# Delta-rule recurrence: four scaling operations read PSUM, and the time rows of k are computed in two other places

## What is computed

```python
q = _causal_dwconv_silu(x @ Wq.T, qcw, qcb).reshape(Bb, Tt, H, DK)
k = _causal_dwconv_silu(x @ Wk.T, kcw, kcb).reshape(Bb, Tt, H, DK) * SCALE
v = _causal_dwconv_silu(x @ Wv.T, vcw, vcb).reshape(Bb, Tt, H, DV)
a = jax.nn.sigmoid(x @ Wa.T + ba).reshape(Bb, Tt, H, DV)
beta = jax.nn.sigmoid(x @ Wb.T + bb)

def step(S, inp):
    qt, kt, vt, at, bt = inp
    err = jnp.einsum('bhij,bhj->bhi', S, kt) - vt
    S = at[..., None] * S - bt[..., None, None] * (err[..., None] * kt[:, :, None, :])
    o = jnp.einsum('bhij,bhj->bhi', S, qt)
    return (S, o)
...
_, o = lax.scan(step, S0, xs)
```

## Time and profile before

| | us |
|---|---|
| median of 3 runs | 3798.8 (3794.1 to 3808.3) |
| the profiled execution | 3802.3 |
| its span | 3800.5 |
| of it the recurrence | about 149 to 2237 |

### The profile page before, as it was taken

One profiled execution on the slowest core, in us unless ns is written; L12 is line 12 of the kernel. 1 busy time (PEld: TensorE's weight loads), 2 busy tenths in 40 slices (PEclk: granted clock), 3 DMA queues, 4 the chain that ended last, 5 costly groups with the idle time before them and its releaser, 6 DMA issues. The chain is left out here.

```text
span 3800.5 us, 141833 instructions
## 1 busy us (share of the span) xinstructions
PE 3221.9 (85%) x61117; PEld 2418.8 (64%) x61117; DVE 2951.2 (78%) x6533; ACT 1981.8 (52%) x4486; POOL 2230.6 (59%) x2825
## 2 busy tenths in 40 slices
PE   3688898888888888889888845689999799889989
PEld 2567676767767676767677644556666477656765
DVE  4488888888888888889888942178888688738884
ACT  2434444444444444444444323258887699629972
POOL 1377778787877777787877744320101388418860
PEclk7889999999999998999999966899999899999999
DMA  2111111111111111111111115100000012101111
GB/s 76 34 43 41 35 52 30 52 34 45 42 45 42 45 41 37 50 30 49 31 40 40 40 31 149 40 1 2 2 2 2 23 35 44 29 20 29 43 32 28
DMA packets 156019, 141.03 MB, mean 37 GB/s; under 512 B 64976, under 2 KB 108236, under 8 KB 155138
## 3 DMA queue, kind: packets, MB, share of 16 engines
q1 hardware_dynamic: 153090, 129.25, 12.5%
q0 software_dynamic: 2304, 2.71, 0.2%
HBM read 96.12 MB, written 16.82 MB: 30 GB/s over the span
## 5 line engine op out<-in xcount | busy, mean ns | idle before, releaser
L1327 DVE TENSOR_TENSOR a_tmp<-a_h,banks 128x128 f32<-128x128 f32 (+6 forms) x896 | 435.7, 486 | 28.7
L1333 DVE TENSOR_REDUCE a_h<-a_tmp 128x64 f32<-128x128 f32 (+6 forms) x896 | 432.1, 482 | 8.8
L1012 POOL TENSOR_TENSOR a_st<-a_st,a_ab 128x512 f32<-128x512 f32 x252 | 313.6, 1277 | 0.0
L820 ACT ACTIVATE a_kq<-banks 128x512 f32<-128x512 f32 (+2 forms) x160 | 88.3, 552 | 426.6 <-PE banks L556 426.6
L2207 ACT ACTIVATE c_s<-c_s,c_low 128x384 f32<-128x384 f32 (+1 forms) x512 | 266.3, 579 | 19.1 <-DVE c_low L2151 13.6
L1027 POOL TENSOR_TENSOR a_h<-a_h,a_a 128x128 f32<-128x128 f32 (+3 forms) x256 | 141.3, 552 | 228.4 <-DVE a_h L1333 225.6
L2252 POOL TENSOR_TENSOR c_qm<-c_qT,c_heads 128x512 f32<-128x512 f32 x32 | 33.3, 1040 | 396.2 <-PE banks L2076 395.9
L2151 DVE CUSTOM_DVE_ANT_0 c_s<-banks,c_band 128x384 f32<-128x384 f32 (+1 forms) x512 | 245.4, 517 | 23.5 <-PE banks L2076 23.5
L556 PE MATMUL banks<-a_xseg,a_w_q 128*128 128x128 f32 x2048 | 253.4, 278 | 9.0 <-ACT a_kq L820 8.5
L556 PE MATMUL banks<-a_xseg,a_w_k 128*128 128x128 f32 x2048 | 243.0, 276 | 17.1 <-DMA a_xseg<-xn 17.1
L556 PEld LDWEIGHTS banks<-a_xseg,a_w_q 128*128 128x128 f32 x2048 | 235.8, 190 | 21.6 <-ACT a_kq L820 15.4
(11 more groups left out here) (326 smaller groups left out, 8917.5 us busy)
## 6 DMA issues: line engine op xcount, KB each, us to landing
a_ab<-decays SPq DMA_DIRECT2D x512, 128.0 KB, 3.1
d_Vs<-d_V SPq DMA_DIRECT2D x128, 128.0 KB, 2.4
sent<-k_nothing SPq DMA_DIRECT2D x40, 64.5 KB, 2.6
b_xe<-sent SPq DMA_DIRECT2D x8, 322.5 KB, 3.5
a_xseg<-xn SPq DMA_DIRECT2D x32, 70.0 KB, 2.8
a_xrow<-in_L_attn_x SPq DMA_DIRECT2D x128, 16.0 KB, 1.8
x<-a_xrow SPq DMA_DIRECT2D x128, 16.0 KB, 1.8
back<-k_nothing SPq DMA_DIRECT2D x32, 64.0 KB, 1.6
```

The source lines that it names most:

```text
L1012: e.tensor_tensor(sv, sv, self.ab[:, 8 * n:8 * n + 8, :], ALU.mult).then_inc(*self.s_decay.at((g, n)))
L1327: e.tensor_tensor(prod, both, gram, ALU.mult).then_inc(*step.at((g, t, "product")))
L1333: e.tensor_reduce(self.results(ch, t), prod, AX.X, ALU.add).then_inc(*step.at((g, t, "w")))
```

## The change

It does four things, all in `DeltaRule`.

1. Gram rows. The rows of bank 2 are kept in another order, q of step t-1 before k of step t, and only in the columns that the products read: columns 0 to 7 for the steps of the first half, 8 to 15 for those of the second. Two copies of 112 and 120 elements take the place of two of 240 and 256. The column of outputs O moves to the front of H, so that one sum still writes both results.
2. Factors. In the columns of bank 2 that are now free ScalarE copies the dk of rows 0 to 3 and 8 to 11 (`act_factors`, two copies of 128 elements), before the Gram rows of the same chunk. It waits for GpSimd's dk and for the last chunk's line 1391. GpSimd waits for this copy before it overwrites dk, where it waited for the multiplications.
3. Products. The multiplications of lines 1297 and 1363 read the factor in PSUM and write their product to unread columns of bank 3; the subtraction and addition behind them (lines 1302 and 1366) read it there. Line 1297 now waits for the factors and for the gate rows of its chunk.
4. Time rows. `pe_time_rows` and `act_time_rows` leave the beginning of a segment. Half 0 stands ahead of the second chunk's `pe_cross`, half 1 between the two halves of v's projection. The last segment has none.

The core of the diff:

```diff
@@ layouts
-            self.W = [self.H[:, :, ch * SEG:(ch + 1) * SEG] for ch in range(NCK)]
-            self.Wx, self.O = self.H[:, :, 2 * SEG:2 * SEG + CK], self.H[:, :, 2 * SEG + CK:]
+            self.O, self.Wx = self.H[:, :, 0:CK], self.H[:, :, CK + 2 * SEG:]
+            self.W = [self.H[:, :, CK + ch * SEG:CK + (ch + 1) * SEG] for ch in range(NCK)]
...
-        self.gbank = c.bank(2).rearrange("p (t z j) -> p t z j", z=2, j=CK)
+        self.gbank = c.bank(2).rearrange("p (r j) -> p r j", j=CK)
+        self.factor = [self.gbank[:, 2 * HC * h:2 * HC * (h + 1), HC - HC * h:CK - HC * h].rearrange("p r (i t) -> p r i t", t=HAND)
+                       for h in range(2)]
+        self.scaled = c.bank(3)[:, HAND * 32:2 * HAND * 32].rearrange("p (r i t) -> p r i t", i=2, t=HAND)
@@ act_gram_bank, act_factors
-        e.activation(self.gbank[:, 0:CK - 1, 0, :], self.g2[:, 1:CK, 0, js], ACT.Copy)
-        e.activation(self.gbank[:, :, 1, :], self.g2[:, :, 1, js], ACT.Copy).then_inc(*self.s_gbank.at(g))
+        e.activation(self.gbank[:, 0:2 * HC - 2, 0:HC], rows[:, 1:2 * HC - 1, c0:c0 + HC], ACT.Copy)
+        e.activation(self.gbank[:, 2 * HC:2 * CK - 1, HC:], rows[:, 2 * HC + 1:, c0 + HC:c0 + CK], ACT.Copy).then_inc(*self.s_gbank.at(g))
+
+    def act_factors(self, e, q, g):
+
+        q.wait_ge(self.s_dk, (g, 1))
+        if g:
+            q.wait_ge(self.s_step, (g - 1, "last", "q"))
+        for h in range(2):
+            t = e.activation(self.factor[h], self.by_pairs(self.dk[:, :, h * HC:h * HC + HAND]), ACT.Copy)
+        t.then_inc(*self.s_factor.at(g))
@@ pool_prepare
-            q.wait_ge(self.s_prep, (g - 1, "mul"))
+            q.wait_ge(self.s_factor, g - 1)
             q.wait_ge(self.s_rest, (g - 1, "late"))
-            q.wait_ge(self.s_mid, (g - 1, "mul"))
@@ dve_steps
-        q.wait_ge(self.s_dk, (g, 1))
-        first = P2[:, :, 0:HAND, 0]
-        e.tensor_tensor(first, first, self.dk[:, :, 0:HAND], ALU.mult).then_inc(*self.s_prep.at((g, "mul")))
+        q.wait_ge(self.s_factor, g)
+        q.wait_ge(self.s_abank, g)
+        pairs = self.by_pairs
+        e.tensor_tensor(self.scaled, pairs(P2[:, :, 0:HAND, 0]), self.factor[0], ALU.mult).then_inc(*self.s_prep.at((g, "mul")))
...
-        e.tensor_tensor(Wc[:, :, c0:c0 + HAND], self.bv[:, :, c0:c0 + HAND], first,
+        e.tensor_tensor(pairs(Wc[:, :, c0:c0 + HAND]), pairs(self.bv[:, :, c0:c0 + HAND]), self.scaled,
                         ALU.subtract).then_inc(*self.s_prep.at((g, "sub")))
         q.wait_ge(self.s_prep, (g, "sub"))
         q.wait_ge(self.s_gbank, g)
-        q.wait_ge(self.s_abank, g)
@@ dve_cross
-        e.tensor_tensor(x, x, self.dk[:, :, HC:HC + HAND], ALU.mult).then_inc(*self.s_mid.at((g, "mul")))
+        e.tensor_tensor(self.scaled, pairs(self.X[:, :, HC:HC + HAND, 0]), self.factor[1], ALU.mult).then_inc(*self.s_mid.at((g, "mul")))
...
-        e.tensor_tensor(self.history(ch, HC)[:, :, HC:HC + HAND], self.P2[:, :, HC:HC + HAND, 0], x, ALU.add).then_inc(
+        e.tensor_tensor(pairs(self.history(ch, HC)[:, :, HC:HC + HAND]), pairs(self.P2[:, :, HC:HC + HAND, 0]), self.scaled, ALU.add).then_inc(
@@ tensor
-            for n in range(2):
-                self.pe_time_rows(e, q, s, n)
...
+                self.pe_time_rows(e, q, s, 0)
             self.pe_cross(e, q, s, 1)
             if more:
                 self.pe_project_rows(e, q, "v", nxt, 0)
                 self.pe_past_state(e, q, g + 2)
+                self.pe_time_rows(e, q, s, 1)
                 self.pe_project_rows(e, q, "v", nxt, 1)
```

More of the change, by code:

```diff
@@ L502, in __init__ @@
         self.s_y, self.s_scaled, self.s_cum, self.s_bv, self.s_bg = (sig(n) for n in ("y", "scaled_o", "cum", "bv", "bg"))
+        self.s_factor = sig("factor")
         self.s_p2, self.s_prep, self.s_step, self.s_wt, self.s_st, self.s_o = (
@@ L526, in results @@
     def results(self, ch, t):
-        w, o = self.first_column(ch, t + 1) + t, 2 * SEG + CK + t - 1
-        return self.H[:, :, w:o + 1:o - w].rearrange("p i z -> p z i")
+        w, o = self.first_column(ch, t + 1) + t, t - 1
+        return self.H[:, :, o:w + 1:w - o].rearrange("p i y -> p y i")
     def ubank(self, n):
@@ L886, in act_gram_bank @@
         s, ch = divmod(g, 2)
-        js = slice(ch * CK, (ch + 1) * CK)
+        c0, rows = ch * CK, self.g2[:].rearrange("p t z j -> p (t z) j")
         q.wait_ge(self.s_bg, (s, ch))
@@ L890, in act_gram_bank, with by_pairs @@
             q.wait_ge(self.s_step, (g - 1, "last", "q"))
-        e.activation(self.gbank[:, 0:CK - 1, 0, :], self.g2[:, 1:CK, 0, js], ACT.Copy)
-        e.activation(self.gbank[:, :, 1, :], self.g2[:, :, 1, js], ACT.Copy).then_inc(*self.s_gbank.at(g))
+        e.activation(self.gbank[:, 0:2 * HC - 2, 0:HC], rows[:, 1:2 * HC - 1, c0:c0 + HC], ACT.Copy)
+        e.activation(self.gbank[:, 2 * HC:2 * CK - 1, HC:], rows[:, 2 * HC + 1:, c0 + HC:c0 + CK], ACT.Copy).then_inc(*self.s_gbank.at(g))
+    def by_pairs(self, x):
+        return x.rearrange("p (r i) t -> p r i t", i=2)
+    def act_factors(self, e, q, g):
[5 more added lines that the diff above has]
+        t.then_inc(*self.s_factor.at(g))
     def act_out(self, e, q, s):
@@ L946, in scalar @@
         self.act_cross_gram(e, q, 0)
+        self.act_factors(e, q, 0)
         self.act_gram_bank(e, q, 0)
@@ L956, in scalar @@
                     self.act_project_rows(e, q, "a", nxt, half)
-            for n in range(2):
-                self.act_time_rows(e, q, s, n)
             if older >= 0:
@@ L969, in scalar @@
                     self.act_project(e, q, "q", nxt, part)
+            self.act_factors(e, q, g + 1)
             self.act_gram_bank(e, q, g + 1)
@@ L983, in scalar @@
                     self.act_next_gram(e, q, s, n)
+                self.act_time_rows(e, q, s, 0)
             if old >= 0:
@@ L987, in scalar @@
                 self.act_cross_gram(e, q, nxt)
-                for half in range(2):
-                    self.act_project_rows(e, q, "v", nxt, half)
-            if more:
+                self.act_project_rows(e, q, "v", nxt, 0)
+                self.act_time_rows(e, q, s, 1)
+                self.act_project_rows(e, q, "v", nxt, 1)
+                self.act_factors(e, q, g + 2)
                 self.act_gram_bank(e, q, g + 2)
@@ L1037, in past_part @@
     def past_part(self):
-        return self.H[:, :, SEG:SEG + CK]
+        return self.H[:, :, CK + SEG:CK + SEG + CK]
     def pool_past(self, e, q, s):
@@ L1046, in pool_past @@
         q.wait_ge(self.s_wm, 2 * s + 1)
-        e.tensor_tensor(self.past_part(), self.H[:, :, 0:CK], by, ALU.mult).then_inc(*self.s_past.at(s))
+        e.tensor_tensor(self.past_part(), self.W[0][:, :, 0:CK], by, ALU.mult).then_inc(*self.s_past.at(s))
     def pool_clear(self, e, q, s):
@@ L1313, in dve_steps @@
             both = hist[:, :, lo:t + 1].rearrange("p (o i) j -> p o i j", o=1).broadcast_to([P, 2, 32, t + 1 - lo])
-            gram = self.gbank[:, t - 1, :, lo:t + 1].rearrange("p z (o j) -> p z o j", o=1).broadcast_to([P, 2, 32, t + 1 - lo])
+            gram = self.gbank[:, 2 * t - 2:2 * t, lo:t + 1].rearrange("p y (o j) -> p y o j", o=1).broadcast_to([P, 2, 32, t + 1 - lo])
             if t == lo + 1 and lo:
@@ L1337, in dve_cross @@
     def dve_cross(self, e, q, s, ch):
-        g, x = 2 * s + ch, self.X[:, :, HC:HC + HAND, 0]
+        g, pairs = 2 * s + ch, self.by_pairs
         q.wait_ge(self.s_step, (g, HC - 1, "w"))
@@ L1389, in dve_state @@
             e.transpose(self.Wt[:].rearrange("p x i -> p i x"), Wc).then_inc(*self.s_wt.at(g))
-        gq = self.gbank[:, CK - 1, 1, HC:].rearrange("p (o j) -> p o j", o=1).broadcast_to([P, 32, HC])
+        gq = self.gbank[:, 2 * CK - 2, HC:].rearrange("p (o j) -> p o j", o=1).broadcast_to([P, 32, HC])
         e.tensor_tensor(self.tmp[:, 1, :, 0:HC], Wc[:, :, c0 + HC:row], gq, ALU.mult).then_inc(*self.s_step.at((g, "last", "q")))
```

2 lines of the change are left out of this document (1 added, 1 removed).

## The result

The changed kernel takes 3707.2 us (median of 4 runs, 3700.7 to 3721.1) against 3798.9 us before: a ratio of 0.976, 95% interval 0.973 to 0.979. That is 92 us faster, where 159 us were forecast.

What follows compares the result with a forecast made beforehand. Bound by VectorE's own work plus two round trips through TensorE. Gains 82 (operations) + 119 (waits) - 25 (new wait) = 176 us, less 15 for longer waits, 161: 3802 to 3641, said 3640 us; range 3605 to 3715.

Steps and rivals of the forecast that it cites:

- The four operations: VectorE lines 1297, 1302, 1363, 1366 each fall to 289 ns with one PSUM operand: 82 us over 64 chunks.
- The reason given, waiting for GpSimd: VectorE's operations with two SBUF operands run long because they wait inside the instruction for GpSimd, not from computing.
- Time rows and the clock: Moved time rows fill TensorE's idle time before second cross and line 691; full clock at both, first-chunk waits 0.
- What is then late: VectorE's waits left after the move: 0.96 us at second cross, 0.67 at second past chunk, 52 us over 32 segments.
- the 0.96 us of the full-clock row: VectorE's wait behind the second chunk's cross at 457.38, run at full clock, taken as what stays there.
- gone: 119: VectorE's waits for cross and past-chunk matmuls fall from 170.8 us to 52, a gain of 119 us.
- rival 1: TensorE's clock stays at the lower level behind shorter gaps, costing 50 us: 3690 us, 15%.
- longer waits in some segments that I see no reason to lose: Mean segment 0.48 us longer than the one followed: 15 us in all, taken off the 176 us gain.
- Rival 2: Time rows become late ahead of the second cross, where only 0.35 us are idle; 32 us lost: 3672 us, 12%.
- The new wait: VectorE waits before line 1297 for ScalarE's factors and gate rows: 0.8 us in 31 first chunks, 25 us lost.
- the prediction's path: Check between line 1348's starts: 29.3 us first to second chunk, 30.8 second to first.
- the forecast of 60.1 us a segment: Path check of the recurrence: 60.1 us a segment against 65.2 in the mean, 160 us over 31.5 segments.

Runs made afterwards that it cites:

- e1: The changed kernel with both halves of k's time rows back at their old place, Gram rows, factors and products staying changed: 3730.5 us, ratio 0.980.
- e4: The changed kernel with the 32 small matmuls of each next-Gram half replaced by one 128x352 matmul, output not the reference's: 3675.1 us, ratio 0.964.
- e7: The changed kernel with time rows half 0 behind q's projection and the output projection between the halves of the next Gram product: 3663.8 us, ratio 0.961.
- e5: The changed kernel with the output projection between the two halves of the next Gram product instead of ahead of both: 3694.5 us, ratio 0.969.
- e11: The changed kernel with each matmul of the time rows split into two of half the columns: 3745.3 us, ratio 0.985.

## Why the prediction came out as it did

**The four operations: right.** Forecast 82 us, measured 81.0; e1, which has this part alone, is 2.0% or 75 us faster. The surcharge of 65 ns for a PSUM operand that the Trainium skill would add (VectorE: DVE Perf Modes, "The TRN2 errata") is not seen: 287 to 296 ns against the 289 of the earlier trace rows, and lines 1297, 1302 and 1363 with their two SBUF operands took 291 or 292 ns at the fastest.

The reason given, waiting for GpSimd, is borne out by an operation that was not changed. Line 1417, which writes the outputs (1398 before), has two SBUF operands and took 0.69 us each time in the kernel before. In the change VectorE comes to it earlier, and in 8 of 64 cases it takes 0.99 to 1.29 us, each time beside GpSimd's making of dk. One of them:

```profile
1389.62 1.07 POOL L1082 TENSOR_TENSOR a_dk<-a_dc,a_beta 128x448 f32<-128x448 f32 x1
1390.04 1.20 DVE L1417 TENSOR_TENSOR a_o<-a_p,a_h 128x512 f32<-128x512 f32 x1
1390.62 0.78 POOL L1084 COPY a_dk<-a_beta 128x64 f32<-128x64 f32 x1
```

VectorE ends 0.55 us after GpSimd's 1082 (1390.69), and GpSimd's 1084 in turn takes 0.78 us instead of 0.31 and ends 0.16 us after VectorE. The Trainium skill says so (SBUF — State Buffer, "Who interferes with whom"): an instruction of VectorE with two SBUF inputs contends with a GpSimd instruction that reads SBUF, and the second one waits for the first to end; with at most one SBUF input it doesn't. The traces agree in both halves: the 0.55 us that VectorE goes on behind GpSimd's 1082 are nearly its own 0.69, and the four operations with one SBUF operand took 286 to 297 ns in all 256 cases. It cost 4.0 us of the gain here.

**Time rows and the clock: half right.** The first chunk's crosses came to 0.39 us (forecast 0, before 1.27), the past chunk in first chunks to 0.00 as forecast, and the clock stays up in all but 4 second crosses. The next first cross, which before began 0.8 us late and without idle time, begins at 1031.79 after 0.47 us in which TensorE waited for VectorE.

**What is then late: the step that failed.** "In the second chunk the 0.96 us of the full-clock row stays" was 3.42 us, 2.46 x 32 = 79 us of the missing gain; the first crosses' 0.39 us are another 12, and the 0.97 in place of 0.67 at the past chunk 10. That is 101 us, which is what "gone: 119" lacks against the 18 measured. (The operations' 81 and these 18, less 4.0 for line 1417, make 95 us, the difference of the two profiled spans, 3800.5 and 3705.2.) I had taken the time rows as a block of 1.01 us that fills an idle time of 2.30, and looked only at which semaphore ends last. The idle time was doing something: instructions arrived in it. The trace of before showed it, as stops marked issue of 12.5 us inside line 709 and 16.7 inside line 735. The 0.96 us itself was a choice of row: before, the second cross ran at full clock in 11 segments, in 4 of them VectorE waited 0.96 or 0.97 us, and in the other 7 the cross was stopped for 1.3 to 2.0 us and VectorE waited 2.7 to 5.5. The prediction says in rival 1 that "TensorE's records have gaps of their own", puts 15 us down to "longer waits in some segments that I see no reason to lose", and does not ask what the gaps were. Rival 2 named the place ("any gap of TensorE delays the cross"), at 1 us a segment instead of 2.5 and with 12%. That the time lies in the range all the same is partly luck: the range was drawn round rivals with smaller losses, and 25 us of the loss were made up by a wait that did not come.

A page of the Trainium skill bears on this, and I had not weighed it (Runtime: NRT & Kernel Launch, "Instruction fetch mechanics"): instructions come in blocks of 16 KiB, 256 of them, by a queue that the sequencer drives itself. The 256 records a packet, and the place of all 866 stops, agree. It also says that crossing a block's end is "mostly hidden". In the change 273 of 370 crossings were without a stop above 0.3 us, but the 97 others are 94 us in sum (50 before), and the ones in the second cross stand on the path that sets the time.

**The new wait: right in size, and not there.** 0.8 us were forecast in 31 chunks. In the change VectorE comes too late to meet it. Where the stops are taken away it is there, 0.6 to 0.7 us in 18 chunks of e4 and 20 of e7. The intervals from second to first line 1348 are then 31.0 to 31.1 us in 16 of 31 segments of e4; the prediction's path gave 30.8. The 17 segments of e4 whose second cross waits 0.97 or 0.98 us take 59.6 to 61.4 us, 60.4 in the median. So the forecast of 60.1 us a segment is about right for segments in which TensorE has its instructions at that cross. Over all segments e7 comes to 60.9, the change to 62.2.

**What spaces the long stops.** Longer stops come at a regular distance: in the change at lines 587 and 638 at 371, 681, 931, 1180, 1429, 1677 and 1990 us, four or five segments apart, and the long second-cross waits of e4 come every fourth or fifth segment. The records give the reason. A segment of the change has 3011 of them, 61 short of 12 blocks, so the block ends stand 61 records later in each next segment and one is back at the same place after 256 / 61 = 4.2 segments. In e4 a segment has 2763, 53 short of 11 blocks, and 256 / 53 = 4.8. What is slow is not a certain block but the place in the segment on which a block's end falls.

**Open.** Why a packet comes when it does, and never within 3.2 us of the last, no run tests. GpSimd's chain as the next bound was not shortened in any run.

## What to carry to other kernels

- Idle time on TensorE ahead of a run of small matmuls may be the time in which its instructions arrive. Before filling it, count the matmuls and weight loads of the run: here a new 256 never came sooner than 3.2 us after the last, and a run of 576 that would take 4.3 us was stopped once or twice in 29 of 31 segments. A single fast block can pass (28 of the change's took under 3.2 us and did not end in a stop), but no two in a row passed without a stop in under 6.7 us. Put long matmuls between short ones (e5: the same work, 0.7% faster; e7, with the time rows moved too, 1.5%), and count rows marked issue as a term of the sum.
- To find out whether such stops are for instructions, number the engine's records and look whether all stops leave the same remainder by 256.
- An operation of VectorE with two SBUF operands beside a busy GpSimd took up to 1.1 us more than at its fastest (line 1297 before, 292 to 1407 ns). Where one operand can lie in PSUM that is gone, but the next such operation on the chain may run into the same neighbour once VectorE is earlier.

## What the runs showed of the hardware

- All 866 stops of TensorE marked issue in the recurrence of 12 traces stand at the same place of a block of 256 records, and end 2.2 to 3.4 us after a 16 KB packet of the instruction queue; two such packets are there at least 3.2 us apart.
- 248 instructions less a segment in the same time took 20 us of stops out of the cross (e4), 128 more put 36 us of stops in (e11).
- GpSimd and VectorE held each other up in both directions: 0.69 to 1.20 us and 0.31 to 0.78 us in one meeting.
